# A mixture-of-experts stage that scatters its output rows into token order on GpSimd, and a next loop that loads them with plain transfers

## The chip, the cores and the metric

The program runs on one core of one Trainium2 chip. The metric is the device time of one execution in microseconds (us); the number quoted is the median of several runs. The engines are TensorE (PE in the profile, with its weight loads as PEld), VectorE (DVE), ScalarE (ACT), GpSimd (POOL) and SyncE (SP). SP and ACT can queue plain DMA transfers; POOL can queue indirect ones, whose row addresses come from a list in SBUF.

## What is computed

The reference runs two blocks on a tensor of 32 images x 256 channels x 14 x 14. The change lies in the feed-forward part of block 0 (a top-2 mixture of 32 experts) and at the start of block 1. Cut to what matters:

```python
def _L0_ffn_ref(x, router_w, expert_weights):        # x: tokens x 256
    rw = jax.nn.softmax(logits, axis=-1).reshape(T, E)
    vals, idx = jax.lax.top_k(rw, 2)
    # out = sum over the two chosen experts e of  w_e * (x @ W_e)
...
x = x + conv0(layernorm_c(x))                        # sections a, b, c
t = tokens(x); t = t + _L0_ffn_ref(layernorm_t(t))   # router, experts
x = x + squeeze_excite(layernorm_c(x))               # next loop
t = tokens(x); t = t + moe1(layernorm_t(t))          # next loop, then the long last loop
```

There are 32 x 196 = 6272 tokens, so 12544 pairs of a token and a chosen expert.

## The kernel before, in words

The kernel is one program of blocks that follow one another with a barrier between them. Token chunks hold 392 tokens (two images); there are T = 16 chunks, each of NSUB = 4 pieces of SUB = 98 tokens. Three blocks matter here.

**The router block (L1146 to L1485).** For each chunk it adds the residual, normalises, turns the tokens into rows (`xnb`, evacuated by ACT in `evacuate`, L1366) and computes router scores. DVE picks the two best experts for a group of two chunks (`best`, `second_best`) and gives each token two row numbers (`slots`, L1293, into `SLOT`) in a table that is sorted by expert. POOL then scatters each piece of 98 rows twice into the DRAM table `xg_d` (L1190), 128 indirect DMAs in all. The table has TILES = 132 tiles of ROWS = 128 rows (each expert's share is filled up to whole tiles, with rows that a block before has set to zero, L926). Two small tensors end the block: PE multiplies `expert_f` by `owned` (L1485), and DVE copies the result into `EID`, the expert of each tile.

**The expert block (L1496 to L1551).** It walks over PAIRS = 66 pairs of tiles, all engines through the helper `staged` (L51), which unrolls four steps and runs the rest in a loop of two steps per turn. For pair t: SP loads the two tiles from `xg_d` into the half t % 2 of `xr` (L1500; it waits until pair t-2 has been transposed); PE transposes them (L1513), ACT evacuates (L1535), and one step later PE multiplies by the weights of each tile's expert, which it looks up in `EID` (L1517, eight matmuls, L1524); DVE copies the products from PSUM into `yr` (L1546); ACT queues the store of the whole pair to `yg_d` (L1537), which keeps the order of the experts. PE's order is: transposes of t, matmuls of t-1, transposes of t+1, and so on. `xr`, `xt`, `yr` and the PSUM tiles have two buffers each.

**The next loop (L1698 to L2074).** For each chunk, POOL fetches the two expert rows of every token from `yg_d` with eight indirect DMAs (L1743 to L1749) into `gath`, which has three buffers. ACT multiplies the first row by its share (`weigh_first`, L1867), DVE adds the second (`weigh_second`, L1753), PE turns the result back (`turn`, L1958), DVE adds it to the residual (`add_experts`, L1763). Then come layer norm, squeeze-and-excite, another layer norm, a linear layer and the second router, spread over six further steps. ACT starts its first chunk only when twelve small weight loads that SP queues have landed (semaphore `H["w"]`, L1933).

Of the kernel before, what the change touches and what calls it, by code (L numbers as in the profile page):

```python
# [81 lines left out]
def build(nc, x, c1T, c2T, c3T, invts, lut1, lut2, lut3, bn1, bn2, bn3, routerT, w_moe,  # L82
          se_w1T, se_b1, se_w2T, se_b2, se_wgT, se_bg, wm, bm, emb, w1, b1, w2, b2, wo, bo, out):
    with ExitStack() as ctx:
# [3 lines left out]
        def sem(name):  # L88
            return nc.alloc_semaphore(name=name)
# [76 lines left out]
        ZF = TILES * ROWS * C // (ZQ * 128)  # L166
        xg_d = nc.dram_tensor("xg_d", [TILES * ROWS, C], F32)
# [896 lines left out]
        yg_d = nc.dram_tensor("yg_d", [TILES * ROWS, C], F32)  # L1064
# [24 lines left out]
        EID = sbd("EID", [1, TILES], U32)  # L1089

# [7 lines left out]
        def sbr(name, shape, dt=F32):  # L1098
# [7 lines left out]
        expert_f = sbr("expert_f", [E0, 1])  # L1106
        xnb = sbr("xnb", [SUB, XB, NSUB, C])
# [22 lines left out]
                                        "rowv", "slot", "own", "eid", "chain", "wm")}  # L1130
# [15 lines left out]
        with nc.Block() as block:  # L1146
# [21 lines left out]
            def _(eng):  # L1168
                eng.memset(before[:], 1.0).then_inc(D["set"], 1)
                eng.iota(iota_i[:, 0:E0], pattern=[[-1, E0]], base=E0, channel_multiplier=0)  # L1170
# [10 lines left out]
                eng.tensor_copy(expert_f[:], iota_i[0:E0, E0 + TILES:])  # L1181
# [16 lines left out]
            def _(eng):  # L1198
# [37 lines left out]
                def best(g):  # L1236
# [3 lines left out]
                    wait(eng, D["exp"], g)  # L1240
                    step(eng.tensor_reduce(mx[:, 0], lgs, AX.X, ALU.max))
# [106 lines left out]
                eng.tensor_copy(EID[:], psP[0:1, 0:TILES])  # L1348

            @block.scalar  # L1350
            def _(eng):
# [14 lines left out]
                def evacuate(f, k):  # L1366
                    if k == 0:
                        wait(eng, d_sc[f % XB], f // XB * 16 * NSUB * 2)
                    wait(eng, D["tr"], 2 * f + k + 1)
                    eng.activation(xnb[:, f % XB, 2 * k:2 * k + 2].rearrange("p s c -> p (s c)"),  # L1370
                                   ps4[0:SUB, 2 * (f % 2) + k], ACT.Copy).then_inc(D["ev"], 1)

                relu(0)
                for s in range(T + GC + 1):
# [20 lines left out]
                    if not placing and g >= 0:  # L1395
# [3 lines left out]
                        eng.activation(mx[:, 5], mx[:, 2], ACT.Exp).then_inc(D["e2"], 1)  # L1399

            @block.tensor
            def _(eng):
# [82 lines left out]
                eng.matmul(psP[0:1, 0:TILES], expert_f[:], owned[:], start=True, stop=True).then_inc(D["eid"], 1)  # L1485
# [3 lines left out]
        X = {k: sem(f"x_{k}") for k in ("tr", "ev", "mm", "y")}  # L1489
# [3 lines left out]
        xr = vv[:].rearrange("p u h c -> p (u h c)")[:, 0:4 * C].rearrange("p (u r c) -> p u r c", u=2, r=2)  # L1493
# [900 lines left out]
```

## Time and profile before

| what | value |
|---|---|
| time, median of 3 runs | 2449.26 us (2446.92 to 2452.71) |
| profiled execution, its own time | 2452.87 us |
| span of its trace | 2451.2 us |
| PE busy | 2084.4 us, 85% |
| DVE busy | 1347.7 us, 55% |
| ACT busy | 1289.6 us, 53% |
| POOL busy | 968.5 us, 40% |
| router block, last scatter issued | at 935 us |
| expert block | 941 to 1148 us |
| next loop | from 1148 to about 1500 us |

The profile page comes from one execution. It gives each engine's busy time, the busy share in 40 slices, the chain of work that ended last, the costliest groups of instructions by source line, and the DMA transfers. The trace behind it can be asked for a stretch in order of time, for one line's instructions and what they waited for, and for busy time and granted TensorE clock in chosen windows. A clock of 1.00 is full speed, 0.50 is half. The starts and durations of matmuls are close, but their ends are modelled.

### The profile page before, as it was taken

The numbers are of one execution on the slowest core, as the hardware profiler recorded it, in microseconds if no ns is written. First come the engines' busy times: TensorE is split into PE (matmuls) and PEld (weight loads), VectorE is DVE, ScalarE is ACT, GpSimd is POOL, SyncE is SP. The second block draws the span as 40 slices with busy tenths as digits, with TensorE's granted clock in tenths as the row PEclk, the third lists the DMA queues.
The fourth block names the chain that finished last, engine by engine and source line by source line (L and its number), as shares of the span: only waits on it lengthen the run. The fifth ranks groups of instructions, "written<-read, shape, count | busy, mean of one in ns | idle before, by whom it ended". The sixth has DMA issues, their size and how long they took to land. (4 is left out here: it accounts for less than half of the span.)

```text
span 2451.2 us, 36445 instructions
## 1 busy us (share of the span) xinstructions
PE 2084.4 (85%) x12850; PEld 1158.6 (47%) x12851; DVE 1347.7 (55%) x2117; ACT 1289.6 (53%) x1634; POOL 968.5 (40%) x673
## 2 busy tenths in 40 slices
PE   6998599997977864775799964999999999999998
PEld 3444355554535544664466542444444444444444
DVE  5666435554458861221566652676666666666633
ACT  2444222222544421111344423888888888898887
POOL 4332111210004772001775002655565656565554
PEclk8999779998897757998698886999999999999999
DMA  2110212210724434555232104556565656565563
GB/s 54 28 33 8 86 46 68 65 64 34 250 62 126 145 98 129 172 172 158 72 106 93 48 33 104 141 143 156 147 172 146 156 149 160 148 159 145 146 157 107
DMA packets 206933, 274.84 MB, mean 112 GB/s; under 512 B 49190, under 2 KB 163446, under 8 KB 206646
## 3 DMA queue, kind: packets, MB, share of 16 engines
q1 hardware_dynamic: 173366, 227.84, 33.6%
q0 software_dynamic: 12288, 25.72, 3.5%
q10 hardware_dynamic: 21120, 19.18, 2.3%
q8 instruction: 98, 1.61, 0.3%
q14 instruction: 61, 0.50, 0.1%
HBM read 203.76 MB, written 68.83 MB: 111 GB/s over the span
## 5 line engine op out<-in xcount | busy, mean ns | idle before, releaser
L2292 ACT ACTIVATE BIG<-psA,b_s 128x1024 f32<-128x1024 f32 x784 | 809.8, 1115 | 127.8 <-PE psA L2233 127.5
L2233 PE MATMUL psA<-x_r,w_r 128*128 128x512 f32 x1568 | 477.9, 427 | 46.8 <-ACT BIG L2292 24.9
L2222 POOL TENSOR_TENSOR BIG<-BIG 128x1024 f32<-128x1024 f32 x147 | 376.6, 2562 | 356.4 <-DVE BIG L2313 222.6
L2313 DVE SCALAR_TENSOR_TENSOR BIG<-psY,b_s,BIG 128x512 f32<-128x512 f32 x392 | 292.1, 750 | 340.4 <-PE psY L2243 261.6
L2233 PEld LDWEIGHTS psA<-x_r,w_r 128*128 128x128 f32 x1568 | 269.3, 190 | 314.5 <-ACT BIG L2292 220.9
L2243 PE MATMUL psY<-BIG,w_s 128*32 128x512 f32 x3136 | 388.0, 607 | 15.9 <-DVE BIG L2313 8.2
L2243 PEld LDWEIGHTS psY<-BIG,w_s 128*32 128x32 f32 x3136 | 80.1, 109 | 214.8 <-issue 132.2
L715 DVE TENSOR_REDUCE b_nm<-psN 112x32 f32<-112x512 f32 x128 | 83.1, 686 | 152.9 <-PE psN L612 152.5
L1191 POOL DMA_INDIRECT xg_d<-xnb,SLOT x128 | 135.0, 1055 | 80.4 <-DVE SLOT L1306 43.9
L1524 PE MATMUL ps<-BIG,xv 128*128 x528 | 132.4, 394 | 39.2 <-ACT xv L1535 29.5
L1748 POOL DMA_INDIRECT gath<-yg_d,SLOT x128 | 137.2, 1072 | 65.8 <-issue 36.9
L553 POOL CAST b_pat_r<-BIG 72x3584 fp32r<-72x3584 f32 x16 | 50.7, 3170 | 224.8 <-PE psN L612 211.9
L1535 ACT ACTIVATE xv<-ps 128x512 f32<-128x512 f32 x66 | 39.4, 597 | 188.9 <-PE ps L1513 188.9
L715 DVE TENSOR_REDUCE a_nm<-psN 98x32 f32<-98x512 f32 x128 | 82.4, 685 | 89.0 <-PE psN L603 88.9
L1524 PEld LDWEIGHTS ps<-BIG,xv 128*128 128x128 f32 x528 | 95.8, 191 | 65.0 <-issue 54.5
L2206 POOL CAST x_r<-xv 128x1024 fp32r<-128x1024 f32 x49 | 51.9, 1059 | 186.8 <-DMA xv<-hs_d 186.6
L2208 POOL TENSOR_TENSOR x_r<-xv,x_r 64x1024 fp32r<-64x1024 f32 x49 | 118.0, 2407 | 3.9
L576 PE MATMUL ps<-BIG,b_wb 72*128 72x392 f32 x256 | 100.6, 539 | 3.5 <-DVE xv L721 3.5
L771 ACT ACTIVATE b_exs<-ps 128x1568 f32<-128x1568 f32 x32 | 47.3, 1477 | 104.3 <-PE ps L581 104.3
L1733 POOL MEMSET embd<- 128x64 f32 x1 | 0.2, 156 | 211.9 <-POOLq L1496 211.9
L612 PE MATMUL psN<-b_wb_r,b_pat_r 73*112 73x128 f32 x512 | 71.1, 286 | 14.8 <-POOL b_pat_r L553 14.0
L612 PEld LDWEIGHTS psN<-b_wb_r,b_pat_r 73*112 73x112 f32 x512 | 61.5, 194 | 35.6 <-POOL b_pat_r L553 14.8
(394 smaller groups left out, 3266.3 us busy)
## 6 DMA issues: line engine op xcount, KB each, us to landing
BIG<-wt_d SPq DMA_DIRECT2D x784, 128.0 KB, 2.8
xv<-hs_d SPq DMA_DIRECT2D x196, 128.0 KB, 3.0
BIG<-ypad_d SPq DMA_DIRECT2D x144, 120.0 KB
xg_d<-ex SPq DMA_DIRECT2D x64, 264.0 KB, 3.8
xv<-xg_d SPq DMA_DIRECT2D x66, 256.0 KB, 2.9
xv<-x SPq DMA_DIRECT2D x64, 196.0 KB, 2.7
yg_d<-ex ACTq DMA_DIRECT2D x33, 256.0 KB, 3.2
yg_d<-sq ACTq DMA_DIRECT2D x33, 256.0 KB, 3.2
```

The source lines that it names most:

```text
L576: eng.matmul(ps4[:, i, 0:CH], w_, src, start=True, stop=False)
L612: mm = eng.matmul(psN[0:SR, bank, g * 128:(g + 1) * 128], pat_r[0:KR, bank * 4 + g, sub * SR:(sub + 1) * SR], wb_r[0:KR, bank * 4 + g], st ...
L715: eng.tensor_reduce(dst, src, AX.X, ALU.max, negate=True).then_inc(S["max"], 1)
L1191: eng.indirect_dma_start(xg_d.ap(), bass.IndirectOffsetOnAxis(ap=SLOT[:, t * NSUB + s, j:j + 1], axis=0), xnb[:, t % XB, s], None).then_in ...
L1524: m = eng.matmul(psZ[:, u, r * C:(r + 1) * C], xt[:, u, r, h * 128:(h + 1) * 128], w_moe_s[:, bass.ds(e * (2 * C) + h * C, C)], start=(h = ...
L1748: eng.indirect_dma_start(gath[:, c % GB, 2 * s + j], None, yg_d.ap(), bass.IndirectOffsetOnAxis(ap=SLOT[:, c * NSUB + s, j:j + 1], axis=0) ...
L2208: eng.tensor_tensor(x_r[64:128, w % 2], stk[64:128, w % 2], x_r[64:128, w % 2].bitcast(F32), ALU.subtract).then_inc(Q["lo"], 1)
L2222: eng.tensor_tensor(gacc[:, w % 2], gacc[:, w % 2], gsum[:, a % 2], ALU.add).then_inc(Q["acc"], 1)
L2233: mm = eng.matmul(psA[m % 3][:, b * BLK:(b + 1) * BLK], w1_r[:, m % 16], x_r[:, w % 2, b * BLK:(b + 1) * BLK], start=True, stop=True)
L2243: mm = eng.matmul(psY[use % 2][32 * e:32 * e + 32, :], w2_s[:, g % 4 * 4 + e], hid[:, (4 * g + e) % 8, b * BLK:(b + 1) * BLK], start=True, ...
L2292: eng.activation(hid[:, m % 8], psA[m % 3][:], ACT.Gelu, bias=b1_s[:, m % 16:m % 16 + 1]).then_inc(Q["gel"], 1)
L2313: eng.scalar_tensor_tensor(out=dst, in0=psY[use % 2][:], scalar=b2_s[:, g % 4:g % 4 + 1], in1=wb[:, g % 3, b * BLK:(b + 1) * BLK], op0=ALU ...
```

## The change

- The row of a token in `xnb` and in `xg_d` grows from C = 256 to CW = 272 floats (1024 to 1088 bytes). Column 256 carries FAR minus twice the token's number, column 257 the code of the token's first expert. ACT writes both in a new function `label`, four small instructions per group of two chunks; the scatter waits for it (`D["id"]`). The zeroing transfers grow alike.
- PE's last matmul of the router block writes the experts of the tiles to all 128 partitions, and DVE makes `rev_tile` from them.
- In the expert block, DVE works out a destination row for every row of a pair, before it copies that pair's products: two `scalar_tensor_tensor` on a column of 128, a wait, and one `tensor_scalar` into `dest`. The result is twice the token's number, plus one where the tile's expert is not the first choice; filler rows get a number out of bounds. SP's load waits for these instructions also (`X["ix"]`), because they read `xr`.
- The stores leave ACT. POOL issues two indirect scatters per pair, of 128 rows each, into `yt_d`, which is in token order. DVE waits for the scatters of pair t-2 before it works on pair t.
- In the next loop POOL's 128 gathers are gone. SP loads a chunk of `yt_d` by one plain transfer: three ahead of its weight loads, five behind them, and from then on one per chunk, eight chunks ahead.

```diff
+        CW = C + 16
-        xg_d = nc.dram_tensor("xg_d", [TILES * ROWS, C], F32)
+        xg_d = nc.dram_tensor("xg_d", [TILES * ROWS, CW], F32)
...
-        yg_d = nc.dram_tensor("yg_d", [TILES * ROWS, C], F32)
+        yt_d = nc.dram_tensor("yt_d", [2 * B * HW, C], F32)
...
                 for t in range(T):
                     wait(eng, D["slot"], t // GC + 1)
                     wait(eng, D["ev"], 2 * (t + 1))
+                    wait(eng, D["id"], t // GC + 1)
...
                 eng.tensor_copy(EID[:], psP[0:1, 0:TILES])
+                eng.tensor_scalar(rev_tile[:], psP[:, 0:TILES], -1.0, float(E0), ALU.mult, ALU.add)
...
+                def label(g):
+                    for i in range(GC):
+                        t = GC * g + i
+                        eng.activation(xnb[:, t % XB, :, C], tok_i[:, t * NSUB:(t + 1) * NSUB], ACT.Copy)
+                        m = eng.activation(xnb[:, t % XB, :, C + 1], mx[:, 1, i * NSUB:(i + 1) * NSUB], ACT.Copy)
+                    m.then_inc(D["id"], 1)
...
             def _(eng):
                 def front(k, t, n, u):
                     wait(eng, X["tr"], t - 1)
+                    wait(eng, X["ix"], t - 1)
                     eng.dma_start(xr[:, u], xg_d.ap()[...]).then_inc(x_ld[u], 16)
...
-                def late(k, t, n, u):
+                staged(eng, front, None, PAIRS, 1)
+
+            @block.gpsimd
+            def _(eng):
+                def late(t, u):
+                    wait(eng, X["ix"], t + 1)
                     wait(eng, X["y"], t + 1)
-                    eng.dma_start(yg_d.ap()[...], yr[u]...).then_inc(x_st[u], 16)
-                staged(eng, front, None, PAIRS, 1, late=late)
+                    for r in range(2):
+                        eng.indirect_dma_start(yt_d.ap(), bass.IndirectOffsetOnAxis(ap=dest[:, u, r:r + 1], axis=0),
+                                               yr[u][:, r * C:(r + 1) * C], None, bounds_check=2 * B * HW - 1, oob_is_err=False).then_inc(x_st[u], 16)
+                for t in range(PAIRS):
+                    late(t, t % 2)
...
             @block.vector
             def _(eng):
                 def back(k, t, n, u):
+                    tile = rev_tile[:, at_chunk(t, 2)]
+                    wait(eng, X["tr"], t + 1)
+                    wait(eng, x_st[u], n * 32)
+                    for r in range(2):
+                        m = eng.scalar_tensor_tensor(out=back_d[:, u, r:r + 1], in0=xr[:, u, r, C + 1:C + 2], scalar=tile[:, r:r + 1],
+                                                     in1=xr[:, u, r, C:C + 1], op0=ALU.is_equal, op1=ALU.add)
+                    m.then_inc(X["id"], 1)
+                    wait(eng, X["id"], t + 1)
+                    eng.tensor_scalar(dest[:, u], back_d[:, u], -1.0, float(FAR + 1), ALU.mult, ALU.add).then_inc(X["ix"], 1)
                     wait(eng, X["mm"], t + 1)
-                    wait(eng, x_st[u], n * 16)
                     eng.tensor_copy(yr[u], psZ[:, u]).then_inc(X["y"], 1)
...
+                def load_experts(c):
+                    wait(eng, H["w0"], c - GB + 1)
+                    wait(eng, H["y"], 2 * (c - GB + 1))
+                    eng.dma_start(gath[:, c % GB]..., yt_d.ap()[2 * c * CH:2 * (c + 1) * CH]...).then_inc(h_g[c % GB], 16)
+
+                AHEAD = 8
+                for c in range(GB):
+                    load_experts(c)
...
+                for c in range(GB, AHEAD):
+                    load_experts(c)
                 for c in range(T):
                     wait(eng, H["hs"], c + 1)
...
+                    if c + AHEAD < T:
+                        load_experts(c + AHEAD)
...
-                            eng.indirect_dma_start(gath[:, c % GB, 2 * s + j], None, yg_d.ap(),
-                                                   bass.IndirectOffsetOnAxis(ap=SLOT[:, c * NSUB + s, j:j + 1], axis=0)).then_inc(h_g[c % GB], 16)
```

## Rows read from the trace of the kernel before

**Rows 1.** Windows: start:end and length us; busy us by engine (instructions), PEclk, DMA share, GB/s.

```profile
941.00:1149.00 208.00, 161.97 (x792) 129.37 (x792) 45.63 (x66) 39.41 (x66) 0.51 (x4) 0.98 0.55 166
```

**Rows 2.** Timeline of one steady stretch: start us, us, engine, line, operation, what it waited for.

```profile
1042.42 0.60 PE L1513 MATMUL ps<-ident,xv 128*128 128x128 f32 x4
...
1043.40 1.99 PE L1524 MATMUL ps<-BIG,xv 128*128 x8 [0.38 <-DVE sq L1550]
...
1045.23 0.60 PE L1513 MATMUL ps<-ident,xv 128*128 128x128 f32 x4
1045.52 0.69 DVE L1550 COPY ex<-ps 128x512 f32<-128x512 f32 x1 [2.12 <-PE ps L1524]
...
1048.56 0.60 PE L1513 MATMUL ps<-ident,xv 128*128 128x128 f32 x4
1048.86 0.69 DVE L1550 COPY sq<-ps 128x512 f32<-128x512 f32 x1 [2.64 <-PE ps L1524]
```

**Rows 3.** Line L1550: durations ns (min, median, max), first and last start.

```profile
L1550 DVE COPY ex<-ps x33: 690/692/692, 949.2 to 1143.0; 128x512 f32<-128x512 f32 x33
L1550 DVE COPY sq<-ps x33: 690/691/692, 951.3 to 1145.0; 128x512 f32<-128x512 f32 x33
```

**Rows 4.** SP's queue in that stretch, then the landing times of line L1501.

```profile
1043.20 0.37 SPq L1501 DMA_DIRECT2D xv<-xg_d  x1
...
DMA to landing us min/median/max: 2.6/2.9/3.9
```

**Rows 5.** Timeline of the router block's end: two small DVE operations, the second dependent.

```profile
916.59 0.20 DVE L1313 RECIPROCAL P<-mx 98x8 f32<-98x8 f32 x1
916.83 0.17 DVE L1314 TENSOR_TENSOR P<-mx,P 98x8 f32<-98x8 f32 x1
```

**Rows 6.** Line L1191: durations ns, first and last start, landing times of its scatters.

```profile
L1191 POOL DMA_INDIRECT xg_d<-xnb,SLOT x128: 952/956/1956, 759.3 to 935.5; - x128
...
DMA to landing us min/median/max: 2.4/2.5/4.6
```

**Rows 7.** The page's list of DMA issues: the store of a pair, us to landing.

```profile
yg_d<-ex ACTq DMA_DIRECT2D x33, 256.0 KB, 3.2
```

**Rows 8.** Timeline of the next loop's start: POOL's last gather of chunk 0, and ACT's first weighing.

```profile
1155.38 0.29 DVE L1826 TENSOR_SCALAR w1t<-w1t 128x256 f32<-128x256 f32 x1 [9.72 <-DMA embd<-emb]
...
1159.91 0.97 POOL L1748 DMA_INDIRECT gath<-yg_d,SLOT  x1 [0.30 <-issue]
...
1163.28 1.70 ACT L1872 ACTIVATE yn<-gath,P 98x256 f32<-98x256 f32 x4 [21.79 <-DMA gath<-yg_d,SLOT]
```

**Rows 9.** Timeline: the expert block's first pairs, at half clock.

```profile
943.73 1.97 PE L1513 MATMUL ps<-ident,xv 128*128 128x128 f32 x8 [25.20 <-DMA xv<-xg_d]
...
945.88 3.26 PE L1524 MATMUL ps<-BIG,xv 128*128 x8 [0.18 <-issue]
```

**Rows 10.** Timeline of the next loop: ACT's squares behind a weighing that waited for gathers.

```profile
1171.80 0.97 DVE L1769 TENSOR_TENSOR BIG<-V,psMO 128x784 f32<-128x784 f32 x1 [3.08 <-PE psMO L1975]
...
1174.41 0.84 ACT L1879 ACTIVATE sq<-BIG 128x784 f32<-128x784 f32 x1
...
1192.43 0.97 DVE L1769 TENSOR_TENSOR BIG<-V,psMO 128x784 f32<-128x784 f32 x1 [1.25 <-PE psMO L1975]
...
1195.85 0.84 ACT L1879 ACTIVATE sq<-BIG 128x784 f32<-128x784 f32 x1
```

**Rows 11.** Windows in the expert, the router and the next block (columns as in Rows 1).

```profile
953.00:956.00 3.00, 1.48 (x10) 1.10 (x9) 0.69 (x1) 0.60 (x1) 0.00 (x0) 1.00 0.75 202
...
741.00:941.00 200.00, 129.15 (x686) 97.16 (x684) 138.72 (x369) 60.78 (x118) 135.04 (x128) 0.66 0.38 116
...
1154.00:1160.00 6.00, 0.00 (x0) 0.00 (x0) 0.39 (x2) 0.00 (x0) 4.48 (x6) 0.50 0.93 217
```

**Rows 12.** Timeline: one gather beside a DVE cast from SBUF to SBUF.

```profile
1189.42 1.89 POOL L1748 DMA_INDIRECT gath<-yg_d,SLOT  x1 [0.30 <-issue]
...
1189.97 1.21 DVE L1853 CAST w_r<-BIG 128x2048 fp32r<-128x2048 f32 x1
```

More of the change, by code:

```diff
@@ L1089, in build @@
         EID = sbd("EID", [1, TILES], U32)
+        rev_tile = sbd("rev_tile", [128, TILES])
+        FAR = 1 << 20
+        back_d = sbd("back_d", [128, 2, 2])
+        dest = sbd("dest", [128, 2, 2], U32)
         GC = 2
@@ L1129, in build @@
                                         "tr", "lgd", "ev", "dl", "exp", "top", "e2", "mask", "tot", "rank", "rhsn", "nb", "rhsv", "rows",
-                                        "rowv", "slot", "own", "eid", "chain", "wm")}
+                                        "rowv", "slot", "own", "eid", "chain", "wm", "pad", "id")}
         d_ld = [sem(f"d_ld{u}") for u in range(2)]
@@ L1240, in best @@
                     wait(eng, D["exp"], g)
+                    wait(eng, D["id"], g)
                     step(eng.tensor_reduce(mx[:, 0], lgs, AX.X, ALU.max))
@@ L1369, in evacuate @@
                     wait(eng, D["tr"], 2 * f + k + 1)
-                    eng.activation(xnb[:, f % XB, 2 * k:2 * k + 2].rearrange("p s c -> p (s c)"),
-                                   ps4[0:SUB, 2 * (f % 2) + k], ACT.Copy).then_inc(D["ev"], 1)
+                    eng.activation(xnb[:, f % XB, 2 * k:2 * k + 2, 0:C],
+                                   ps4[0:SUB, 2 * (f % 2) + k].rearrange("p (s c) -> p s c", c=C), ACT.Copy).then_inc(D["ev"], 1)
+                def label(g):
[4 more added lines that the diff above has]
+                    m.then_inc(D["id"], 1)
+                eng.wait_ge(D["pad"], 2)
                 relu(0)
@@ L1484, in _ @@
                 eng.wait_ge(D["own"], 1)
-                eng.matmul(psP[0:1, 0:TILES], expert_f[:], owned[:], start=True, stop=True).then_inc(D["eid"], 1)
+                eng.matmul(psP[:, 0:TILES], expert_b[:], owned[:], start=True, stop=True).then_inc(D["eid"], 1)
         r_ctx.close()
-        X = {k: sem(f"x_{k}") for k in ("tr", "ev", "mm", "y")}
+        X = {k: sem(f"x_{k}") for k in ("tr", "ev", "mm", "id", "ix", "y")}
         x_ld = [sem(f"x_ld{u}") for u in range(2)]
@@ L1742, in _ @@
                                       base=-32 * r, pattern=[[-1, HD]], channel_multiplier=1).then_inc(Q["set"], 1)
-                for c in range(T):
-                    wait(eng, H["w0"], c - GB + 1)
-                    wait(eng, H["y"], 2 * (c - GB + 1))
-                    for s in range(NSUB):
-                        for j in range(2):
-                            eng.indirect_dma_start(gath[:, c % GB, 2 * s + j], None, yg_d.ap(),
-                                                   bass.IndirectOffsetOnAxis(ap=SLOT[:, c * NSUB + s, j:j + 1], axis=0)).then_inc(h_g[c % GB], 16)
             @block.vector
@@ L1753, in weigh_second @@
                 def weigh_second(c):
-                    wait(eng, h_g[c % GB], (c // GB + 1) * 16 * NSUB * 2)
+                    wait(eng, h_g[c % GB], (c // GB + 1) * 16)
                     wait(eng, H["w0"], c + 1)
@@ L1867, in weigh_first @@
                 def weigh_first(c):
-                    wait(eng, h_g[c % GB], (c // GB + 1) * 16 * NSUB * 2)
+                    wait(eng, h_g[c % GB], (c // GB + 1) * 16)
                     wait(eng, H["tr"], c - 1)
```

21 lines of the change are left out of this document (13 added, 8 removed).

## The prediction, made before the changed kernel was run

> **What bounds the kernel now.** I read the windows first, to see how full each engine is in the blocks that change, then one steady stretch in order of time, then the queue of SP. In the expert block PE is busy 162 of 208 us at a granted clock of 0.98 [rows 1]: PE sets the pace and the rest follows. The reader should see in the stretch [rows 2] that the transposes of a pair start at 1042.42, 1045.23 and 1048.56, so two pairs take 6.14 us, and that DVE's copy of a pair starts 3.10 us (1045.52 - 1042.42) or 3.63 us (1048.86 - 1045.23) after the transposes of the next pair. Over the whole block the copies start every (1145.0 - 949.2) / 65 = 3.01 us [rows 3]. The load of the pair after next leaves SP at 1043.20, which is 0.78 us after the transposes that free its buffer began, that is some 0.18 us after they ended [rows 2, 4]. It lands 2.9 us later, near 1046.1, and is wanted at 1048.56: 2.4 us of slack. That slack is what the change spends.
>
> **The expert block, part by part.**
>
> *The load's new wait.* The load of pair t now waits for the destination numbers of pair t-2. DVE works them out after its copy of pair t-3, as its instructions run in order. That copy waits for the matmuls of t-3, which PE does after the transposes of t-2. Behind SP's wait only the next load is queued, and PE waits for that. The laps are: transposes of a pair to the end of the copy of the pair before, (3.10 + 3.63) / 2 + 0.69 = 4.06 us [rows 2]; the destination numbers; SP's step, 0.18; the load, 2.9 and 0.05 for PE to see it. The numbers are two tiny operations, of which the second follows half covered, and a third that depends on them. Small DVE operations take 0.17 to 0.20 us, and a dependent one starts 0.24 us after the one before [rows 5]; I take 0.6 us in all with register work for the loop's addresses, bounds 0.4 and 0.8 (the trace has no such chain with register addresses). Sum: 4.06 + 0.6 + 0.18 + 2.95 = 7.79 us for two pairs, 3.90 us per pair instead of 3.01.
>
> *The store's new path.* Before it works on pair t, DVE waits for the scatters of pair t-2, so the numbers of t-2 also wait for the scatters of t-4. POOL's indirect DMA takes 0.96 us, and the next starts 0.30 us later [rows 6, 8]. Both are queued after the copy, so the second starts 0.1 + 1.26 us after it. When it lands is not shown for a scatter of 128 rows: the scatters of 98 rows landed 2.4 to 4.6 us after their start, median 2.5 [rows 6]. The last gather of chunk 0 started at 1159.91 and ACT used it at 1163.28, 3.4 us later [rows 8]. The plain store of a pair takes 3.2 [rows 7] against 2.9 for a load. I take 3.6 us, nearest to the gather, plus a little as it writes DRAM, and keep 2.5 and 4.6 as the ends. The store's lap is then 0.1 + 1.26 + 3.6 = 4.96 us. The circle through it spans three pairs: 4.06 + 4.96 + 0.6 + 0.18 + 2.95 = 12.75 us, 4.25 us per pair. It is longer than the 3.90 of the load's circle alone, so it decides. At a landing of 2.5 us both circles give 3.9, and at 4.6 the longer gives 4.6. POOL itself needs 2 x 1.26 = 2.5 us per pair; if its work went by rows (128 for 98) it would need 3.1. Neither is the bound, though the second adds some 0.6 us to the store's lap and 0.2 to the period.
>
> *Sum.* (4.25 - 3.01) x 64 = +79 us; ends +57 (3.90) and +102 (4.6). The unrolled first pairs run into the same waits; only the first two are left out. At the block's end the store's 3.2 us become 4.96: +2.
>
> *A shared port.* One gather took 1.89 instead of 0.97 us beside a DVE cast between two SBUF tiles that ran from 1189.97 for 1.21 us [rows 12]. The Trainium skill's page "SBUF — State Buffer", section "Who interferes with whom", says that DVE in a two-port mode holds the pair of ports that GpSimd needs to write descriptors, and that the later one blocks fully; the trace agrees, by that pair of rows. By that rule DVE's big copy, which reads PSUM, should not hold POOL up, and the new tiny operations could cost the store's lap at most their own half microsecond. It is inside the range.
>
> **The router block.** ACT gets four small instructions per group, about 0.9 us in 20, on an engine that is busy 61 of 200 us [rows 11]. They follow the group's scores by a step in which DVE still works on ranks, so POOL's new wait ends before that for `SLOT`: nothing. If that cover were gone it would be 8 x 0.9 = 7 us. `rev_tile` is made while POOL still scatters its last rows. POOL is the bound here: 128 x 1.26 = 161 us of the 176 between its first and last scatter [rows 6]. I cost its longer rows at nothing, since its time per transfer is the same for a gather and a scatter, 0.97 and 0.96 [rows 6, 8]; if it went by bytes it would be 6% of 128 x 0.96, +7 us. The zeroing transfers grow by 6%, a hundred microseconds before anyone waits for them: nothing.
>
> **The next loop.** POOL's eight gathers per chunk, 10.1 us, are gone, but only the first chunks waited for them: the first weighing waited until 1163.28. The new loads do not start it much earlier. SP queues three chunks of 0.80 MB ahead of some 0.5 MB of weights (`w1t`, `w2t` and `wm_s` above all), and ACT waits for these weights. The window from 1154 to 1160 moved 217 GB/s at a DMA share of 0.93 [rows 11]. At that rate 2.9 MB take 13.5 us from 1149, so ACT starts at 1162 to 1163; before, the weights were there by 1155.38 [rows 8]. So the copy's gain is about 1 us, with ends of +2 and -4. Later the weighing of chunk 1 no longer holds up ACT's square, which waited from 1172.77 (the end of DVE's subtraction) to 1174.41, 1.6 us; the same at chunk 3, from 1193.40 to 1195.85, 2.4 us [rows 10]. With a last short wait of chunk 4 I take -6 in all, ends 0 and -12. From chunk 5 on the gathers were hidden by PE and DVE, and removing them brings nothing. SP's new waits stand ahead of its stores of `hs` and `ex`, three steps before anyone needs a chunk; nothing.
>
> **Total.** +79 + 2 + 0 - 6 = +75 us. Made on the profiled execution it is 2452.9 + 75 = 2528; the median of the runs is 3.6 us below that execution, so the forecast is 2525 us.
>
> **The rivals.**
> 1. *Only the load's circle binds.* The scatters land in the 2.5 us that is their median. The period is 3.90: +57 + 2 - 6 = +53, 2502 us. For it speaks the median of rows 6, against it the gather's 3.4 us.
> 2. *PE's clock falls.* PE would be at work 2.6 (0.60 + 1.99) of 4.25 us, 61%, where now it is 2.6 of 3.01. The block's first pairs at half clock took 1.97 us for eight transposes and 3.26 for eight matmuls [rows 9], against 0.60 for four and 1.99 [rows 2]. That lengthens the 4.06 us lap by 1.7, so the longer circle becomes 14.4 us for three pairs, 4.80 per pair: +115 + 2 - 6, 2560 us if it holds throughout, and anything between for a part. For it speaks the router block: busy 129 of 200 us, and the clock was 0.66 on average. Against it, three microseconds of this very block with PE busy 1.48 ran at 1.00 [rows 11]. The Trainium skill's page "TensorE: Matmul & The Clock Gate", section "HAM oscillation — how this bites in real kernels", says that a loop in which PE waits for a DMA at every tile can be throttled again at every tile; no row here shows it for waits as short as 1.2 us.
> 3. *The new wait is hidden, and the change is faster.* The place is the same load. The numbers of pair t-2 are ready 0.69 + 0.6 us after 1045.52, SP issues at 1046.99, and the transposes of t start at 1048.56. Below a landing of 1.5 us the load would still be in time, the period would stay 3.01 and only the gains would be left: +2 - 6, 2445 us. The shortest landing of 66 loads was 2.6 us [rows 4], so this needs numbers that DVE makes ahead of its copy, which its order forbids.
>
> **How the numbers follow.** The forecast (period 4.1 to 4.5, 2510 to 2541) gets 0.45, rival 1 0.22, rival 2 0.24, rival 3 0.03; 0.06 is left for a longer scatter or a cost in POOL's longer rows. The range takes in the load's circle with its shortest terms (numbers 0.4, landing 2.7: 3.7 us per pair, so +44 + 2 - 9) and the clock's case at full length with half of what the store's upper end (landing 4.6) would add to it, some 12 us: 2486 to 2575. A difference of 0.2% (5 us) is about what a measurement can tell from no change. Faster 0.03; same 0.02, where gains and a shorter circle would have to meet; slower 0.95.
>
> **What would show it.** The changed profile should show the block of pairs at 265 to 295 us instead of 208; PE waiting before its transposes for the load of `xr`, 1 to 1.5 us in each pair, where it now never does; SP's load leaving about 0.8 us after the end of DVE's copy, or later, after the scatters' landing; POOL busy about 2 us per pair with idle time behind DVE; ACT's wait of 21.79 us at the next loop's start [rows 8] still there in its greater part, and none for `gath` after it. It would be wrong if the transposes started every 3.0 us with no wait for the load, if POOL's scatter of 128 rows took much over 2 us, or if the next loop shrank by far more than 12 us.

## The result and the profile after

| | before | after | forecast |
|---|---|---|---|
| time, median of the runs | 2448.1 us (2446.8 to 2452.7) | 2560.0 us (2548.7 to 2563.9) | 2525 us (2486 to 2575) |
| ratio to before, 95% interval | | 1.0444 (1.0413 to 1.0475) | 1.031 |
| span of the profiled execution | 2451.2 us | 2558.6 us | |
| expert block, first load to the next block's first load | 207.3 us | 320.0 us | 265 to 295 |
| period of a pair | 3.01 us | 4.68 us | 4.25 |
| from the next block's first load to the end | 1302.9 us | 1293.6 us | 6 less |

The ratio is taken from runs of both kernels on one chip, here and in the experiments. The change makes the kernel 4.4% slower. The direction and the range held; the block of pairs, 320 us, lies outside the 265 to 295 that the prediction gave for it. The forecast is 35 us too low, and some 28 us of that lie in one number, the period of a pair (0.43 us times 65). The 107.4 us between the spans split in this way: the expert block starts 3.9 us later (944.95 for 941.04), takes 112.8 us longer, and what follows it is 9.3 us shorter.

First the copies of the expert block after the change (durations in ns, first and last start), which answer to [rows 3]:

```profile
L1588 DVE COPY ex<-ps x33: 691/692/693, 953.4 to 1255.4; 128x512 f32<-128x512 f32 x33
L1588 DVE COPY sq<-ps x33: 690/692/693, 955.6 to 1257.4; 128x512 f32<-128x512 f32 x33
```

65 periods lie between the first and the last start: (1257.4 - 953.4) / 65 = 4.68 us. Before it was 3.01. The difference, 1.67 us times 65, is 108 of the block's 113 us.

Next the windows of the middle of the block, 1000 to 1130: before, then after. The columns are those of [rows 1].

```profile
1000.00:1130.00 130.00, 103.22 (x512) 82.39 (x511) 29.72 (x43) 25.67 (x43) 0.00 (x0) 1.00 0.56 170
```

```profile
1000.00:1130.00 130.00, 85.58 (x323) 61.09 (x324) 32.52 (x108) 16.12 (x27) 53.02 (x55) 0.86 0.36 114
```

PE is no longer the engine that sets the pace: it is busy 86 of 130 us instead of 103, and no other engine is close to full either. POOL is at 53 of 130. A block in which every engine and the DMA queues have room is paced by a circle of waits. The granted clock is 0.86 where it was 1.00, so part of the block now runs at the lower of its two levels, 1.2 instead of 2.4 GHz.

The list of waits of the block names the links (engine, operation, line and what it waited for: sum, count, longest; L48 is the helper that issues every wait):

```profile
SPq L48 <- DVE dest L1586: 255.4, 64, 5.2
PE ps L1536 <- DMA xv<-xg_d: 76.2, 39, 25.3
DVE back_d L1582 <- DMA yt_d<-sq,dest: 20.7, 15, 2.4
DVE back_d L1582 <- DMA yt_d<-ex,dest: 19.1, 18, 2.5
```

SP waits for the destination numbers ahead of 64 loads. PE waits for the load in 39 places, the first of them the block's start, and DVE for the scatters of `sq` or `ex` in 15 + 18 = 33: in about half of the 66 pairs, not in all. The timeline shows the three together (start, us, what it waited for):

```profile
1084.97 0.69 DVE L1588 COPY ex<-ps 128x512 f32<-128x512 f32 x1 [2.18 <-PE ps L1547]
1086.11 0.63 PE L1536 MATMUL ps<-ident,xv 128*128 128x128 f32 x4 [1.17 <-DMA xv<-xg_d]
1086.79 0.97 POOL L1568 DMA_INDIRECT yt_d<-ex,dest  x1 [1.37 <-issue]
1087.02 0.35 DVE L1582 SCALAR_TENSOR_TENSOR back_d<-xv,rev_tile 128x1 f32<-128x1 f32 x2 [1.36 <-DMA yt_d<-sq,dest]
1087.41 0.35 DVE L1586 TENSOR_SCALAR dest<-back_d 128x2 uint32<-128x2 f32 x1
1087.75 1.99 PE L1547 MATMUL ps<-BIG,xv 128*128 x8 [1.02 <-ACT xv L1558]
1088.07 0.98 POOL L1568 DMA_INDIRECT yt_d<-ex,dest  x1 [0.30 <-issue]
1089.78 0.69 DVE L1588 COPY sq<-ps 128x512 f32<-128x512 f32 x1 [2.02 <-PE ps L1547]
1091.31 0.97 POOL L1568 DMA_INDIRECT yt_d<-sq,dest  x1 [2.27 <-DVE sq L1588]
1091.43 0.63 PE L1536 MATMUL ps<-ident,xv 128*128 128x128 f32 x4 [1.69 <-DMA xv<-xg_d]
1093.06 3.43 PE L1547 MATMUL ps<-BIG,xv 128*128 x8 [1.00 <-ACT xv L1558]
1096.53 0.69 DVE L1588 COPY ex<-ps 128x512 f32<-128x512 f32 x1 [4.25 <-PE ps L1547]
```

```profile
1087.98 0.37 SPq L1524 DMA_DIRECT2D xv<-xg_d  x1
```

The copy that starts at 1084.97 ends at 1085.66. DVE then stands still until 1087.02, waiting for the scatters of the pair before. The numbers are ready at 1087.76, SP's load leaves at 1087.98 and PE's transposes start at 1091.43, after a wait of 1.69 us. The eight matmuls that started at 1087.75 took 1.99 us at a granted clock of 1.00. The next eight, the same work, took 3.43 at 0.57, so most of them ran at the lower level.

Read pair by pair, the trace shows slow matmuls and waits taking turns. In 25 of the block's pairs the matmuls took 2.9 us or longer, and none of these left PE waiting over 0.5 us ahead of its next transposes; after each of the 37 others that could be followed it did wait, 0.5 to 2.3 us. The slow matmuls filled time in which PE would have stood idle.

The scatters themselves, which answer to [rows 6] (durations in ns, then the times to landing):

```profile
L1568 POOL DMA_INDIRECT yt_d<-ex,dest x66: 972/974/1010, 955.0 to 1258.2; - x66
DMA to landing us min/median/max: 2.1/2.5/3.9
```

Last the start of the next loop, which answers to [rows 8]: SP's first loads and ACT's first weighing.

```profile
1264.98 1.35 SPq L1742 DMA_DIRECT2D gath<-yt_d  x3
1282.03 3.30 ACT L1916 ACTIVATE yn<-gath,P 98x256 f32<-98x256 f32 x8 [28.96 <-DMA embd<-emb]
```

ACT starts 17.0 us after the block's end, where before it was 15.0.

### The profile page after: what moved, and what is told of

Same layout as the page of the kernel before. It is cut to its first block and busy times, and to the rows that moved or that the text cites. A ratio compares the mean times of both kernels' runs of the same rounds, so it can differ in the third digit from the quotient of the medians.

```text
span 2558.6 us, 36901 instructions
## 1 busy us (share of the span) xinstructions
PE 2125.5 (83%) x12850; PEld 1179.1 (46%) x12851; DVE 1376.4 (54%) x2316; ACT 1293.6 (51%) x1666; POOL 963.1 (38%) x679
## 5 line engine op out<-in xcount | busy, mean ns | idle before, releaser
L2287 PE MATMUL psY<-BIG,w_s 128*32 128x512 f32 x3136 | 382.1, 599 | 13.5 <-DVE BIG L2373 5.8
L1547 PE MATMUL ps<-BIG,xv 128*128 x528 | 164.7, 466 | 49.7 <-ACT xv L1558 42.8
L1547 PEld LDWEIGHTS ps<-BIG,xv 128*128 128x128 f32 x528 | 114.7, 228 | 83.8 <-issue 65.9
L1536 PE MATMUL ps<-ident,xv 128*128 128x128 f32 x264 | 47.4, 310 | 77.3 <-DMA xv<-xg_d 76.2
L1568 POOL DMA_INDIRECT yt_d<-ex,dest x66 | 64.4, 975 | 99.9 <-DVE dest L1586 66.6
L1568 POOL DMA_INDIRECT yt_d<-sq,dest x66 | 64.3, 974 | 92.9 <-DVE dest L1586 56.4
```

The lines of the kernel that those rows point to most:

```text
L1547: m = eng.matmul(psZ[:, u, r * C:(r + 1) * C], xt[:, u, r, h * 128:(h + 1) * 128], w_moe_s[:, bass.ds(e * (2 * C) + h * C, C)], start=(h = ...
L1568: eng.indirect_dma_start(yt_d.ap(), bass.IndirectOffsetOnAxis(ap=dest[:, u, r:r + 1], axis=0), yr[u][:, r * C:(r + 1) * C], None, bounds_c ...
L2287: mm = eng.matmul(psY[use % 2][32 * e:32 * e + 32, :], w2_s[:, g % 4 * 4 + e], hid[:, (4 * g + e) % 8, b * BLK:(b + 1) * BLK], start=True, ...
```

## Experiments

The numbers of DVE sit in the path of the load because DVE makes them after a copy. The first two runs take apart what of that order costs: the place of the numbers, and the wait for the scatters.

**The numbers ahead of the copy.** DVE makes the numbers of pair t as soon as PE has transposed that pair, before the copy of pair t-1. The numbers of all pairs get a place of their own, so that no new number overwrites one that POOL still reads, and the wait for the scatters stays with the copy.

```diff
-        dest = sbd("dest", [128, 2, 2], U32)
+        dest = sbd("dest", [128, TILES], U32)
...
-                def back(k, t, n, u):
+                def ids(k, t, n, u):
...
-                    wait(eng, x_st[u], n * 32)
...
+                def back(k, t, n, u):
+                    wait(eng, x_st[u], n * 32)
                     wait(eng, X["mm"], t + 1)
...
-                staged(eng, None, back, PAIRS, 1)
+                staged(eng, ids, back, PAIRS, 1)
```

> The changed kernel with DVE's order turned round in the expert block: the destination numbers of pair t are worked out ahead of the copy of pair t-1, into a table with a place for every pair, so they wait for neither that copy nor a scatter; the wait for the scatters stands directly ahead of the copy. POOL's scatters, the wide rows and the plain loads stay. Theory (the 111 us are the load's wait behind copy and scatters, and what the clock loses through it): pairs every 3.0 to 3.1 us, expert block 207 to 215 us instead of 320, clock near 0.98, whole time 2438 to 2452 us. Rival (the scatters themselves, POOL or the DMA engines are too slow for this loop): pairs still every 4.3 us or more, 2530 us or more.

Measured: 2447.5 us, ratio to before 0.9982 (0.9963 to 1.0001). The copies and the window of the middle:

```profile
L1590 DVE COPY sq<-ps x33: 690/692/693, 953.6 to 1138.8; 128x512 f32<-128x512 f32 x33
```

```profile
1000.00:1130.00 130.00, 109.85 (x536) 87.70 (x537) 50.04 (x180) 26.78 (x45) 86.21 (x90) 0.99 0.54 162
```

The first copy starts at 951.1, so the period is (1138.8 - 951.1) / 65 = 2.89 us. PE is busy 110 of 130 us at a clock of 0.99. All of the loss is gone, with the same scatters, the same numbers and the same loads: POOL issues two scatters in each 2.89 us, beside PE at full pace. The loss comes from what stands ahead of the numbers (the copy and the wait for the scatters), and not from what the scatters cost POOL or the DMA engines. The next runs part the copy and the wait.

**The scatters' wait behind the numbers.** The order of after is kept, numbers after the copy. Only the wait for the scatters moves behind the numbers, so the load no longer depends on them.

```diff
-        dest = sbd("dest", [128, 2, 2], U32)
+        dest = sbd("dest", [128, TILES], U32)
...
-                    wait(eng, x_st[u], n * 32)
...
-                    eng.tensor_scalar(dest[:, u], back_d[:, u], -1.0, float(FAR + 1), ALU.mult, ALU.add).then_inc(X["ix"], 1)
+                    eng.tensor_scalar(dest[:, at_chunk(t, 2)], back_d[:, u], -1.0, float(FAR + 1), ALU.mult, ALU.add).then_inc(X["ix"], 1)
+                    wait(eng, x_st[u], n * 32)
                     wait(eng, X["mm"], t + 1)
```

> The changed kernel with only the wait for the scatters moved behind the destination numbers (directly ahead of the copy); the numbers stay behind the copy of the pair before. Theory (two circles, of which the longer goes through the scatters): the load's circle alone is left, 4.06 + 0.5 + 0.2 + 2.75 = 7.5 us for two pairs, 3.75 at full clock and up to 4.1 with the clock as low as in the changed kernel; expert block 250 to 275 us, whole time 2488 to 2515 us. Rival (all of the cost is the scatters' landing): pairs every 3.0 to 3.2 us, 2440 to 2455 us. Rival (the scatters' landing never decided): no change from 2560 us.

Measured: 2562.5 us, 1.0446 (1.0415 to 1.0478); a period of (1260.4 - 952.0) / 65 = 4.74 us. By the median nothing is gained. That is what the recorded rival ("the scatters' landing never decided") forecast, and not the 2488 to 2515 us of the theory. Read as it stands, this says that the circle through the scatters does not bind. But the steps have another shape:

```profile
1105.10 0.69 DVE L1588 COPY ex<-ps 128x512 f32<-128x512 f32 x1 [5.69 <-PE ps L1547]
1107.30 0.69 DVE L1588 COPY sq<-ps 128x512 f32<-128x512 f32 x1 [0.95 <-PE ps L1547]
1109.61 0.63 PE L1536 MATMUL ps<-ident,xv 128*128 128x128 f32 x4 [2.42 <-DMA xv<-xg_d]
1111.20 3.26 PE L1547 MATMUL ps<-BIG,xv 128*128 x8 [0.97 <-ACT xv L1558]
1114.57 0.69 DVE L1588 COPY ex<-ps 128x512 f32<-128x512 f32 x1 [6.03 <-PE ps L1547]
```

The copies come in twos: 2.2 us, then 7.3. PE does two pairs close together, waits 2.42 us for the next load, and the matmuls behind that wait take 3.26 us, mostly at the lower level of the clock. The granted clock of the window from 1000 to 1130 is 0.86, as in after, so the average does not tell the two kernels apart. Either the circle through the scatters does not bind, or its removal is paid back because the slow matmuls now lie in the lap that is left. It took a later experiment to decide.

**The kernel before, with the load behind the copy.** Does the load's dependence cost by itself, with no scatter and no numbers in the kernel?

```diff
                     wait(eng, X["tr"], t - 1)
+                    wait(eng, X["y"], t - 2)
                     eng.dma_start(xr[:, u], xg_d
```

SP's loop was written out step by step for this; its transfers are the same.

> The kernel before with one wait more: SP's load of pair t in the expert block also waits for DVE's copy of pair t-3. SP's loop is written out step by step for that. No wide rows, no labels, no scatter. Theory: the load's circle is 4.06 + 0.2 + 2.75 = 7.0 us for two pairs, 3.5 per pair at full clock; +32 us, up to +55 where the clock falls: 2480 to 2505 us. Rival (the load has slack enough): 2449 us, pairs every 3.0 us.

Measured: 2531.8 us, 1.0322 (1.029 to 1.0355). The copies, the window and the wait (columns as above):

```profile
L1552 DVE COPY sq<-ps x33: 690/691/693, 955.7 to 1228.6; 128x512 f32<-128x512 f32 x33
```

```profile
1000.00:1130.00 130.00, 86.89 (x368) 66.17 (x367) 20.74 (x30) 18.51 (x31) 0.00 (x0) 0.91 0.41 125
```

```profile
PE ps L1515 <- DMA xv<-xg_d: 74.8, 33, 25.2
```

The first copy starts at 953.5, so the period is 4.23 us. The prediction's circle without the numbers is (7.79 - 0.6) / 2 = 3.6; the clock of 0.91 and the hand-overs taken up below are in the difference, which also puts the run above the 2480 to 2505 us expected of it. One wait, put into the old kernel, costs 3.2% of its time and also brings the clock to 0.91. The slack of 2.4 us that the prediction found under the load [rows 2, 4] is spent by this edge, and the rival in which the wait stays hidden is ruled out.

**The next loop alone.** The kernel before, with SP's plain loads of the next loop in place of POOL's gathers. It leaves out the reordering: the rows that it loads are those of the sorted table.

```diff
-                            eng.indirect_dma_start(gath[:, c % GB, 2 * s + j], None, yg_d.ap(),
...
+                AHEAD = 8
+                for c in range(GB):
+                    load_experts(c)
```

> The kernel before with the next loop's part of the change alone: SP loads every chunk by one plain transfer, three chunks ahead of the weight loads, five behind them, one per chunk later; POOL's 128 gathers are gone. The expert block and its stores are those of before, so the rows loaded are those of the sorted table and not the tokens' own: the reordering is left out. Theory (only the first chunks waited for the gathers, and the weights behind three chunks give part of it back): 4 to 10 us less than before, 2441 to 2447 us beside 2451 us. Rival (POOL's gathers held DVE or PE up all through the loop): 15 us less or more.

Measured: 2446.4 us, 0.9982 (0.9968 to 0.9996). From the next block's first load to the end it takes 1296.9 us, against 1302.9 before: 6.0 less. The start of the loop:

```profile
1147.92 1.35 SPq L1704 DMA_DIRECT2D gath<-yg_d  x3
1164.19 3.30 ACT L1879 ACTIVATE yn<-gath,P 98x256 f32<-98x256 f32 x8 [23.06 <-DMA embd<-emb]
```

ACT starts 16.3 us after the block, no earlier than before. The start is bound by the transfers, as the prediction said, and the gain comes later.

**PE kept busy behind its matmuls.** Four, then two, calls of a matmul into `psM`, whose result nobody reads, behind each pair's own matmuls. They were to hold the clock up without delaying the copy.

```diff
                     m.then_inc(X["mm"], 1)
+                    for _ in range(4):
+                        eng.matmul(psM[:, 0:C], mean_w[:], w_moe_s[:, 0:C], start=True, stop=True)
```

> The changed kernel with four matmuls more of 256 columns per pair in the expert block, whose result nobody reads, put behind the pair's own matmuls, where PE waits for a load: some 1.0 us of work per pair at full clock. Theory (the lower clock, 0.85, is a cost of its own on top of the waits): clock 0.95 or more, pairs every 4.2 to 4.3 us, whole time 2528 to 2540 us. Rival (the clock follows the waits and costs nothing of its own): no gain, 2560 us or more.

> The changed kernel with two instead of four unread matmuls more per pair in the expert block, 0.5 us of PE work, so that PE's own work (2.6 + 1.2 + 0.5 = 4.3 us per pair at most) is no longer than the wait it fills. The run with four held the clock at 1.00, but PE's work and gaps came to 4.6 us per pair and were then the bound. Theory (at full clock the load's circle takes 8.2 us for two pairs, the rest of the changed kernel's 9.4 us is the half clock): clock 0.95 or more, pairs every 4.1 to 4.3 us, 2524 to 2538 us. Rival (the low clock costs nothing of its own): 2550 us or more.

Measured: with four calls 2550.3 us, 1.0402 (1.0367 to 1.0436), period 4.50, clock 1.00; with two calls 2550.8 us, 1.0401 (1.0377 to 1.0426), period 4.51, clock 0.97. The windows, four calls and then two:

```profile
1000.00:1130.00 130.00, 117.95 (x570) 98.18 (x569) 35.24 (x113) 16.72 (x28) 54.44 (x56) 1.00 0.40 118
```

```profile
1000.00:1130.00 130.00, 100.08 (x453) 76.96 (x454) 34.29 (x112) 16.72 (x28) 55.46 (x57) 0.97 0.39 117
```

The clock can be held, and both periods are 0.18 us under that of after. But each call became two instructions, so four calls take 1.89 us, where about 1.0 had been planned, and two take 1.03, and they stand ahead of the next transposes. With four, PE is busy 118 of 130 us. Both runs miss the times expected where the clock has a price of its own (2528 to 2540 and 2524 to 2538); the second falls where its rival was put (2550 or more). How much of the clock's gain the calls took back can't be read from these two, so by themselves they are inconclusive on its price.

**PE kept busy where it waits anyway.** In after, PE's matmuls start 1.6 us after its transposes (1086.11 to 1087.75 in the timeline of after), with nothing of PE's between them. PE's sequencer looks up the two experts there. Two calls, 1.03 us, fit into that gap: with them the matmuls still start 1.6 us after the transposes.

```diff
                     m.then_inc(X["tr"], 1)
+                    for _ in range(2):
+                        eng.matmul(psM[:, 0:C], mean_w[:], w_moe_s[:, 0:C], start=True, stop=True)
```

> The changed kernel with two unread matmul calls of 256 columns per pair in the expert block (four instructions, 1.03 us at full clock, as the run with two calls showed), now put directly behind the transposes, where PE stands idle for 1.0 us while its sequencer looks up the experts. There they lengthen nothing: transposes to matmuls stay at 1.6 us. Theory (the half clock in part of the pairs is a cost of its own; at full clock a lap of the load's circle is 1.6 + 2.0 + 0.7 + 0.5 + 0.2 + 3.2 = 8.2 us for two pairs): clock 0.95 or more, pairs every 4.1 to 4.4 us, 2518 to 2542 us. Rival (the clock costs nothing of its own, and the two earlier runs gained by chance): 2552 us or more.

> The same two unread matmul calls in the same place, in the kernel in which the wait for the scatters stands behind the destination numbers. Only the load's circle through the copy is left, at full clock. Theory (both circles are of about one length, 8.2 us for two pairs and 4.3 + 4.7 + 0.5 + 0.2 + 3.2 = 12.9 us for three, and the half clock hid the difference): pairs every 4.1 us, 2512 to 2526 us, and 5 to 15 us below the kernel with the dummies alone. Rival (the scatters never decide): the same time as that kernel within 3 us.

The second of the two makes the same edit on the kernel with the scatters' wait behind the numbers. Measured: on after 2553.7 us, 1.0406 (1.0386 to 1.0426); on the other 2531.4 us, 1.0317 (1.0299 to 1.0335). The windows in that order:

```profile
1000.00:1130.00 130.00, 100.50 (x463) 72.61 (x464) 34.87 (x115) 17.31 (x29) 56.18 (x58) 1.00 0.39 118
```

```profile
1000.00:1130.00 130.00, 104.35 (x495) 78.47 (x496) 33.55 (x120) 18.51 (x31) 60.26 (x62) 1.00 0.42 128
```

Both have the clock at 1.00. Periods by the first and last copy:

```profile
L1590 DVE COPY ex<-ps x33: 691/691/692, 958.5 to 1248.9; 128x512 f32<-128x512 f32 x33
L1590 DVE COPY sq<-ps x33: 691/692/693, 961.5 to 1251.0; 128x512 f32<-128x512 f32 x33
```

```profile
L1590 DVE COPY ex<-ps x33: 691/692/693, 953.9 to 1222.8; 128x512 f32<-128x512 f32 x33
L1590 DVE COPY sq<-ps x33: 691/692/693, 956.9 to 1224.8; 128x512 f32<-128x512 f32 x33
```

(1251.0 - 958.5) / 65 = 4.50 and (1224.8 - 953.9) / 65 = 4.17 us. At the full clock the scatters' wait is worth 0.33 us per pair, 21 us of the block and 0.9% of the whole, and the intervals of the two ratios do not meet. So with the clock held the circle through the scatters is the one that binds, as the prediction had it: between 960 and 1140 DVE then waits for scatters in 35 of 40 pairs, in after in 19 of 38. The first run itself gained little on after. Its 2553.7 us is where its rival was put (2552 or more, the clock costs nothing of its own) and not the 2518 to 2542 of the theory; its ratio of 1.0406 and after's 1.0444 have intervals that overlap. The second missed its 2512 to 2526 us by 5, and gained 22 us on the first where 5 to 15 were expected.

In the earlier run without the scatters' wait the gain was paid back in clock: with the clock held the same kernel falls from 1.0446 to 1.0317, some 31 us. An estimate from the rows gives the size: the load's circle spans two pairs, and with one of its matmuls 1.27 us longer (3.26 for 1.99) it takes 2 x 4.17 + 1.27 = 9.6 us, 4.8 per pair, where 4.74 was measured.

**A version faster than both.** The numbers ahead of the copy, and of the next loop's first three chunks only chunk 0 ahead of the weights.

```diff
-                for c in range(GB):
-                    load_experts(c)
+                load_experts(0)
 ...
+                for c in range(1, GB):
+                    load_experts(c)
```

> The kernel of the first experiment (destination numbers ahead of the copy, whole change else) with the weight loads of the next loop put behind the first chunk's load instead of behind the third's. Theory (ACT's first weighing waits for weights that are queued behind 2.4 MB of chunks, 17 us after the block begins): it starts 9 to 11 us after the block begins, and 5 to 7 us are gained on the first experiment's 2447.5 us: 2440 to 2443 us, below the kernel before. Rival (the start of that loop is set by something else): no change from 2447 us.

Measured: 2435.8 us, 0.9933 (0.9914 to 0.9952). Against the kernel with the numbers ahead of the copy alone, the loop's start shows the reason:

```profile
1150.12 0.36 SPq L1744 DMA_DIRECT2D gath<-yt_d  x1
...
1158.93 1.70 ACT L1919 ACTIVATE yn<-gath,P 98x256 f32<-98x256 f32 x4 [20.80 <-DMA embd<-emb]
```

ACT's first weighing starts 8.8 us after the block's end. With three chunks ahead of the weights it was 17.1. From the next block's first load to the end it takes 1291.0 us, against 1296.1: 5.1 us less. The medians differ by 12 us, more than this accounts for. Where the other 7 come from was not traced; the two were measured on different chips, and their profiled executions have spans of 2442.5 and 2441.1 us.

## Why the prediction came out as it did

**The circle that binds: right with the clock held, half right in after.** The copy, the scatters, the numbers, the load, the next transposes and matmuls form a circle over three pairs, and that was the case the forecast rested on. The pair of runs with the clock held shows it. In after itself DVE waits for the scatters in about half of the pairs, and taking that wait away there gained nothing: the slow matmuls took its place in the lap. One lap of the run on after with the clock held, from the end of a copy to the end of the copy three pairs later:

```profile
1080.48 0.69 DVE L1590 COPY sq<-ps 128x512 f32<-128x512 f32 x1 [2.50 <-PE ps L1549]
...
1083.29 0.97 POOL L1570 DMA_INDIRECT yt_d<-sq,dest  x1 [0.30 <-issue]
...
1086.53 0.35 DVE L1584 SCALAR_TENSOR_TENSOR back_d<-xv,rev_tile 128x1 f32<-128x1 f32 x2 [0.81 <-DMA yt_d<-sq,dest]
1086.91 0.17 DVE L1588 TENSOR_SCALAR dest<-back_d 128x2 uint32<-128x2 f32 x1
...
1090.66 0.63 PE L1536 MATMUL ps<-ident,xv 128*128 128x128 f32 x4 [1.10 <-DMA xv<-xg_d]
...
1092.29 1.99 PE L1549 MATMUL ps<-BIG,xv 128*128 x8
1094.32 0.69 DVE L1590 COPY ex<-ps 128x512 f32<-128x512 f32 x1 [2.52 <-PE ps L1549]
```

| term | predicted | this lap | median of that run | this lap from |
|---|---|---|---|---|
| copy's end to the second scatter's start | 0.1 + 1.26 | 2.12 | 2.11 | 1081.17 to 1083.29 |
| that to the numbers' start, where DVE waited | 3.6 | 3.24 | 2.99 | to 1086.53 |
| numbers | 0.6 | 0.55 | 0.55 | to 1087.08 |
| SP's step and the load, seen by PE where it waited | 0.18 + 2.95 | 3.58 | 0.23 + 3.30 | to 1090.66 |
| transposes to copy's end | 4.06 | 4.35 | 4.34 | to 1095.01 |
| sum | 12.75 | 13.84 | 13.52 | |

The medians add up to three mean periods, 13.5. What they have beyond 12.75 is where the terms were off.

**The step that failed: the sizes of the hand-overs.** Three terms came out too small, and one too large. POOL starts its first scatter 0.84 us after the end of the copy that it waits for (in after, 1090.47 to 1091.31); the prediction had 0.1. PE acts on the load 3.30 us after its issue (3.1 in after, both medians of the pairs in which it waited), where 2.95 was taken from the landing time of 2.9 and 0.05 on top [rows 4]. The transposes stand 1.6 us ahead of the matmuls in every pair of after in which PE had waited, instead of the 0.98 of the first pair in [rows 2]: PE's sequencer looks up the experts between the two. In a full pipeline it does so early (at 1044.90 before, for the transposes of 1045.23); after a wait it begins only behind the first transposes (at 1086.23 in after, for those of 1086.11). Against these, the scatters' landing as DVE sees it was 3.0 instead of 3.6 (2.6 in after). Together they make a period of 4.50 instead of 4.25 us: 0.25 x 65 = 16 us.

**The lower clock: a rival that was half true.** The second rival had the clock fall for the whole block, a period of 4.80. It fell in a part of the pairs: 0.86 on average, the matmuls of a pair at 1.99 or at about 3.4 us. Between after (4.68) and the same kernel with PE's gap filled (4.50) lie 0.18 us per pair in the profiled executions, 12 us of the block. The ratios, 1.0444 and 1.0406, say 9, and as their intervals overlap, the price in after is small and not shown clear of noise. That slow matmuls and waits take turns may be why it is small: a slow pair uses up the wait that would have followed it. The prediction put the case into its range but not into its forecast. The Trainium skill's page "TensorE: Matmul & The Clock Gate", section "HAM oscillation — how this bites in real kernels", which it cited, has the clock throttled again in a loop in which PE waits for a DMA at each tile. The trace agrees in part: PE waited 0.5 to 2.3 us ahead of 38 of its 64 later transposes, and the matmuls right behind 24 of these waits were slow, so it was not every one. The argument against it, three microseconds of the old block at 1.00 with PE busy 1.48 [rows 11], was weak: a single short stretch in a block that otherwise kept PE full.

**The measured time fits the second rival's number, by chance.** The 2560 us measured is the very figure that the prediction gave for the lower clock throughout, and it lies outside the band of the forecast case (2510 to 2541). The block did not get there in that way: 16 us of the 28 that the period lacked come from the hand-overs, which no case of the prediction had, and about 12 from a clock that fell in a part of the pairs. That the range held is owed in part to its room for a clock effect larger than this one. The range's upper end was also added up 3 us too high, 2560 and 12 being 2572; nothing hangs on it.

**The first rival, only the load's circle: wrong.** Its circle measures 4.17 us per pair at full clock where 3.90 was predicted, for the same reasons, and removing the scatters from it gains 0.33.

**The third rival, hidden and faster: wrong for after, and right about what it would need.** The load's wait alone costs 3.2%, 80 us, in the old kernel. The prediction wrote that this case "needs numbers that DVE makes ahead of its copy, which its order forbids". With that order turned round the period is 2.89 and the kernel is level with the old one.

**The block's end: 2 predicted, about 4 measured.** The last scatter in after:

```profile
1260.71 0.98 POOL L1568 DMA_INDIRECT yt_d<-sq,dest  x1 [0.30 <-issue]
```

The last copy ended at 1258.11 and SP went on at 1264.98, 6.9 us later; before it was 2.7 (1145.66 to 1148.32). POOL starts the last pair's two scatters one behind the other, and SP goes on 4.3 us after the second one's start.

**The router block: 0 predicted, about 0 measured.** From the first zeroing transfer to the expert block's first load it is 335.6 us after and 334.9 before. The zeroing starts at 609.3 after and at 606.1 before, so 3.2 of the 3.9 us by which the expert block begins later are there before the first of the changed transfers is issued. They are most likely a difference between two executions: the old kernel with one wait more in the expert block, which has nothing changed ahead of it, began that block at 945.32.

**The next loop: 6 less predicted, 9.3 measured,** and 6.0 in the run with the plain loads alone. The start was forecast 1 us earlier and is 2 later (17.0 us after the block's end for 15.0), within the ends that the prediction gave, so what is gained comes later in the loop. Where it comes, and what makes after's 9.3 more than 6.0, is not traced.

**POOL's longer rows: nothing, as predicted.** 128 rows took 972 to 1010 ns, the 98 rows of the router 952 at the least and 956 in the median [rows 6], and the bound "if its work went by rows" fell. None of the 132 scatters was held up to a length like the 1.89 us of the gather in [rows 12], although 29 of them ran in part beside a copy of DVE out of PSUM (71 with the numbers ahead of the copy, the longest again 1.01 us). The Trainium skill's page "SBUF — State Buffer", section "Who interferes with whom", has a DVE instruction with at most one SBUF input and outside the two-port modes leave GpSimd alone; the trace agrees. What the prediction took from [rows 12] is shown in part: the gather that was held up had started 0.55 us ahead of the cast, so the rows show a hold-up, but not that it is the later one that is held.

**Open.** With the numbers ahead of the copy the expert block is 3.6 us shorter than before (203.7 for 207.3 us). ACT no longer queues the stores there, which may be why; no run tested it.

## What to carry to other kernels

Before a transfer is made to wait for something, work out which instruction the waited-for engine does first in its program order: here a result of two tiny operations stood behind a copy of the last pair and behind a scatter's landing, and that place cost 4.4%, while the same operations one step earlier cost nothing. Sum such a circle with hand-overs as long as engines that really waited show them, here 0.3 to 0.75 us more each than predicted from a full pipeline, and give the clock a term of its own where TensorE comes to wait; how large it is depends on whether the slow matmuls lie in the lap or fill a wait. When the removal of a suspected wait changes nothing, look at the clock before dropping the suspicion, and repeat it with the clock held.

## What the hardware showed that was not expected

- POOL starts an indirect DMA 0.84 us after the end of the DVE copy that it waited for (median of after); SP started a plain load 0.22 us after DVE's last operation. Most of POOL's time is not the wait itself: the copy ended at 1090.47, POOL's sequencer was past its wait at 1090.57, and the scatter began at 1091.31.
- After a wait of its queue PE starts the matmuls 1.6 us after the transposes (1086.11 to 1087.75), for 0.98 in the full pipeline's first pair [rows 2]. The look-up of the experts takes 0.54 us of it in after, from 1086.23.
- An indirect DMA of 128 rows of 1 KB occupies POOL 0.97 us, one of 98 rows 0.96.
- A load that the profile has landing after a median of 2.7 us is acted on by PE 2.9 to 3.5 us after its issue (after, the 38 pairs in which PE waited; median 3.1).
- An average clock does not tell its price. Holding the clock up was worth 4.74 - 4.17 = 0.57 us per pair in the kernel with the scatters' wait moved, and 4.68 - 4.50 = 0.18 in after, where both had an average of 0.86. In the first the slow matmuls lie in the lap of the load; in after they mostly fill a wait.
